# A two-layer decoder on one core: where probabilities, masks and three-part products are computed, and in what order

## The reference

```python
# layer 0: 16 heads of 64
normed = x * rsqrt(mean(x*x) + 1e-6) * norm_w
q, k, v = heads(normed @ wq), heads(ctx @ wk), heads(ctx @ wv)
x = x + (softmax(q @ k.T) @ v) @ wo              # 77 keys, 1024 columns into wo
# layer 1: 16 heads of 16
h = attention(ln1(x), ln1(x), causal=True);  x = x + h @ m_proj + b
h = attention(ln2(x), ctx,    causal=False); x = x + h @ c_proj + b
x = x + relu(ln3(x) @ f_w1 + f_b1) @ f_w2 + f_b2   # 1024 hidden
```

## Time and profile before

| | |
|---|---|
| median of three runs | 5340.66 us |
| profiled execution, its time | 5337.84 us |
| its span | 5336.1 us |
| PE busy | 5106.7 us, 96%, 48328 instructions |
| ACT busy | 4342.2 us, 81% |
| DVE busy | 2212.1 us, 41% |
| POOL busy | 536.4 us, 10% |
| granted TensorE clock, mean | 0.993 |

### The profile page before, as it was taken

The page is one execution under the profiler, slowest core; times in us unless marked ns, Lnnn a source line. Parts: engine busy times, 40 slices in busy tenths (PEclk is TensorE's granted clock), DMA queues, the critical chain, the costliest instruction groups (busy, mean ns, idle before and its releaser), DMA issues.

```text
span 5336.1 us, 138120 instructions
## 1 busy us (share of the span) xinstructions
PE 5106.7 (96%) x48328; PEld 4133.6 (77%) x48328; DVE 2212.1 (41%) x5823; ACT 4342.2 (81%) x17665; POOL 536.4 (10%) x845
## 2 busy tenths in 40 slices
PE   6999999999999999999999999999999999999996
PEld 5777777787787777777777777877777777777775
DVE  3444444443444444444444444434444444444442
ACT  3888888888888888888888888888888888888884
POOL 0001011111111011010110111110110100101100
PEclk9999999999999999999999999999999999999998
DMA  2000000000000000000000000000000000000000
GB/s 76 12 8 14 13 8 13 13 8 13 12 9 13 10 11 13 8 13 13 8 14 13 8 14 13 8 13 10 11 13 8 13 13 8 14 13 7 14 8 5
DMA packets 64257, 67.10 MB, mean 13 GB/s; under 512 B 4593, under 2 KB 62769, under 8 KB 63921
## 3 DMA queue, kind: packets, MB, share of 16 engines
q1 hardware_dynamic: 63920, 64.19, 3.9%
HBM read 47.40 MB, written 16.78 MB: 12 GB/s over the span
## 4 chain that ended last, share of the span: by engine, by line
PE 62%; ACT 24%; DVE 6%; issue 6%; DMA 0%; DVEq 0%; POOL 0%; ACTq 0%; SPq 0%; PEldq 0%; PEld 0%; POOLq 0%
PE ps L876 17%; ACT ps L480 15%; PE ps L841 6%; PE ps L843 5%; PE ps L842 5%; PE ps L1048 5%; PE ps L1031 4%; ACT coT L575 3%; PE ps L1020 3%; PE ps L929 3%; PE ps L1009 2%; PE ps L997 2%; PE ps L939 2%; PE ps L1015 2%; ACT v L460 2%
## 5 line engine op out<-in xcount | busy, mean ns | idle before, releaser
L480 ACT ACTIVATE ps<-ps,negmax 128x77 f32<-128x77 f32 (+2 forms) x6144 | 2076.8, 397 | 197.0 <-DVE negmax L701 195.4
L480 ACT ACTIVATION_READ_ACCUMULATOR ps<-ps,negmax 128x1 f32 x6144 | 1617.6, 275 | 0.8
L701 DVE TENSOR_REDUCE negmax<-ps 128x4 f32<-128x308 f32 (+2 forms) x1792 | 923.5, 563 | 765.8 <-PE ps L939 381.3
L433 POOL TENSOR_TENSOR small<-small 128x1 f32<-128x1 f32 (+1 forms) x448 | 260.9, 582 | 4608.3 <-DVE small L675 2305.7
L696 DVE TENSOR_TENSOR zTl<-ps,zTh 128x256 fp32r<-128x256 f32 x512 | 199.3, 420 | 898.0 <-ACT zTh L460 898.0
L876 PE MATMUL ps<-wf,coT 128*128 128x256 f32 x2048 | 475.8, 386 | 46.4 <-ACT coT L575 46.4
L876 PEld LDWEIGHTS ps<-wf,coT 128*128 128x128 f32 x2048 | 379.8, 190 | 127.0 <-issue 80.2
L876 PE MATMUL ps<-wo,coT 128*128 128x256 f32 x2048 | 475.9, 385 | 0.0
L557 ACT ACTIVATE probs<-ps 128x512 f32<-128x512 f32 x768 | 394.9, 601 | 70.1 <-PE ps L1020 70.1
L876 PEld LDWEIGHTS ps<-wo,coT 128*128 128x128 f32 x2048 | 378.6, 190 | 66.7 <-issue 10.3
L549 ACT ACTIVATE probs<-ps 77x512 f32<-77x512 f32 x512 | 275.5, 588 | 182.2 <-PE ps L981 179.1
(11 more groups left out here) (181 smaller groups left out, 10798.5 us busy)
## 6 DMA issues: line engine op xcount, KB each, us to landing
xin<-x_dram SPq DMA_DIRECT2D x64, 256.0 KB, 2.7
x<-x_dram SPq DMA_DIRECT2D x64, 256.0 KB, 2.7
out<-xr SPq DMA_DIRECT2D x64, 256.0 KB, 2.3
cin<-ctx_dram SPq DMA_DIRECT2D x64, 77.0 KB
wk<-wk_dram SPq DMA_DIRECT2D x1, 1024.0 KB, 5.1
wo<-wo_dram SPq DMA_DIRECT2D x1, 1024.0 KB, 7.9
wf<-f_dram SPq DMA_DIRECT2D x1, 1024.0 KB, 10.3
probs<-wq_dram SPq DMA_DIRECT2D x1, 1024.0 KB, 9.6
```

The costliest lines, as they stand in the source:

```text
L433: nc.gpsimd.tensor_tensor(rstd[:, stage, ts], veps[:, stage, ts], minus_half[:, ts], ALU.pow).then_inc(rstd_ready[stage], 1)
L480: ins = nc.scalar.activation(scores, scores, ACT.Exp, bias=negmax[w][:, t, h:h + 1], accum_out=sums[w][:, t, h:h + 1])
L701: nc.vector.tensor_reduce(dst, bank(s)[:, 0:heads * width].rearrange("p (h k) -> p h k", h=heads), AX_X, ALU.max, negate=True).then_inc(ma ...
```

## The change

Six things change together.

1. Layer 0. `qs0` keeps its exponentials: once ACT has them and their sums, DVE takes the reciprocals of the four sums (128x4) and multiplies the 4x77 probabilities by them, out of PSUM into SBUF. A new step `tr0.t.g` turns four heads over on PE (four transposes of 128x77) and ACT copies them. `ln.0`, `mt.0` and `sk0` are gone.
2. Causal masks. PE's mask matmuls are gone; DVE adds `causal` or `causalT` into the bank in place, and the maxima (by query) or ACT's exponentials (by key) wait for that.
3. `wo` and `f2` become three-part products (24 fp32r matmuls a tile instead of 8 fp32 ones). `pv0`'s result is split by ACT (high) and DVE (low). `h` moves from ACT to DVE: a maximum for the high part, a maximum and subtraction for the low part; `f_b1` is folded in by the bound `minus_bias` and a changed last row of biases.
4. The two weights, in two parts each, share one place in SBUF. Their parts are made at the start, stored to DRAM, and loaded from there in turn, by POOL: 2 MB after `f2` of a turn, 2 MB after `wo`.
5. Each step names its banks. ACT and DVE have orders of their own, in which single banks of a step can stand apart.
6. SP issues its transfers in the turn's order; the last full turn is written out behind the loop.

The diff, cut to its core:

```diff
+pv.1.1:3 rms+ qs0.0.3-:7 qs0.1.3-:6 proj.1.0:0 proj.1.1:4 tr0.1.1-:3 stat.2.0 tr0.1.0-:0 v0.1-:2 stat.2.1
+...
+        def load_parts(kind):
+            n = "wo0" if kind == "wo" else "f2"
+            nc.gpsimd.dma_start(tail_h[:], parted[n][0]).then_inc(tail_in[kind], 16)
+            nc.gpsimd.dma_start(tail_l[:], parted[n][1]).then_inc(tail_in[kind], 16)
+        pool.wait_ge(parts_out, 64)
+        load_parts("wo")
...
+                    if n in ("wo", "f2") and (n, 1 - step[1]) in c.seen:
+                        done = {s: v for st in order if st[0] == n for s, v, _ in c.of[st]["bank"]}
+                        for s, v in done.items():
+                            pool.wait_ge(full[s], v)
+                        ...
+                            load_parts(later[0])
...
+            def mask(u, r, heads, tile, at, added):
+                s, v, _ = u["bank"][r]
+                dve.wait_ge(full[s], v)
+                scores = bank(s).rearrange("p (h k) -> p h k", h=heads)[:, :, at:at + P]
+                nc.vector.tensor_tensor(scores, scores, tile[:].unsqueeze(1).to_broadcast([P, heads, P]),
+                                        ALU.add).then_inc(added, 1)
...
                     elif n == "qs0":
+                        if r == 0:
+                            maxima(u, 0, negmax[0][:, t, hs], 4, S)
+                            continue
+                        dve.wait_ge(summed_up, u["summed"][0][2])
+                        link(u, 0, nc.vector.reciprocal(over[:, t, hs], sums[0][:, t, hs]))
+                        nc.vector.tensor_tensor(rows_of_four(t, g)..., bank(s)..., over[...], ALU.mult).then_inc(free[s], 1)
...
-                        for s, _, _ in u["bank"]:
-                            diagonal = bank(s).rearrange("p (h k) -> p h k", h=heads)[:, :, 512 // heads - P:]
-                            pe.matmul(diagonal, identb[:], causal[:]..., start=False, stop=True, ...)
...
-                    elif n == "sk0":
-                        ...
+                    elif n == "tr0":
+                        for j in range(4):
+                            ins = pe.transpose(bank(s)[0:S, j * P:(j + 1) * P], rows_of_four(t, g)[:, j * S:(j + 1) * S],
+                                               ident[:])
...
+            def tail_product(u, th, tl, t):
+                for k in range(M0):
+                    ins = three(bank(s)[:, 0:C], th[:, k, ts], tl[:, k, ts], tail_h[:, k, :], tail_l[:, k, :],
+                                k == 0, k == M0 - 1)
+                    elif n == "h":
+                        ins = nc.vector.tensor_scalar(hTh[:, k, :], bank(s)..., minus_bias[:, k:k + 1], None, ALU.max)
+                        ins = nc.vector.scalar_tensor_tensor(out=hTl[:, k, :], in0=bank(s)..., scalar=minus_bias[:, k:k + 1],
+                                                             in1=hTh[:, k, :]..., op0=ALU.max, op1=ALU.subtract)
```

More of the change, by code:

```diff
@@ L44 @@
[L44 to L48, removed]
@@ new lines @@
+turn.1.0 turn.1.1 sk2.0/0 sk2.0/3 sk2.0/1 sk2.1/1 sk2.0/2 sk2.1/3 sk2.1/0 sk2.1/2 q1.1 pv.2.0 pv.2.1 k1 ck cv
+ctx qsA/2 turn.3.0 q0.2 qsA/0 k0.1 turn.3.1 qsA/3 qsA/1 qsB.1/3 qsB.1/1 k0.0 qsB.1/2 qsB.1/0 qs0.0.0 q0.1
+qsB.0/3 qsB.0/0 qsB.0/1 qsB.0/2 tr0.0.0 ln.1 qs0.0.1 v1 v0.0 mt.1 qs0.1.1 tr0.0.1 qs0.0.2 skB/3 skB/0 skB/2
+skA.0/3 skA.0/2 skA.0/0 skA.0/1 skB/1 qs0.1.0 qs0.1.2 pv.1.0 skA.1/0 skA.1/3 skA.1/2 skA.1/1
+"""
+DVE_ORDER_TEXT = """
+rms pv.1.1 qs0.0.3/0 qs0.1.3/0 proj.1.0 proj.1.1 stat.2.0 qs0.0.3/1 stat.2.1 norm.2.0 qs0.1.3/1 norm.2.1
@@ new lines @@
+norm.0 pv0.1 turn.2.0 turn.2.1 pv0.0 turn.0 qs2.1/3 pv0.2 qs2.1/0 qs2.1/2 qs2.1/1 pv0.3 qs2.0/3 qs2.0/2
+qs2.0/1 qs2.0/0 wo.0 stat.1.0 norm.1.0 wo.1 stat.1.1 ln.2 norm.1.1 turn.1.0 turn.1.1 pv.2.0 pv.2.1 proj.2.0
+stat.3.0 proj.2.1 stat.3.1 norm.3.0 qsA/m2 qsA/2 qsA/m0 ctx qsA/0 norm.3.1 qsA/m3 turn.3.0 qsA/m1 qsA/3 qsA/1
+turn.3.1 qsB.1/m3 qsB.1/m1 qsB.1/3 qsB.1/1 qsB.1/m2 h.3/0 h.3/1 qsB.1/2 qsB.1/m0 qsB.1/0 qsB.0/m3 qsB.0/m0
+qs0.0.0/0 qsB.0/m1 qsB.0/m2 qsB.0/3 qsB.0/0 qs0.0.0/1 qsB.0/1 qsB.0/2 h.2/0 h.0/0 qs0.0.1/0 h.0/1 h.2/1 ln.1
@@ L135, in next @@
-    def next(self, step):
[L136 to L154, removed]
+        self.after = after
+        self.of = {step: {"place": k, **{r: [None] * n for r, n in USES[step[0]].items()}} for k, step in enumerate(order)}
+        self.seen = set()
+        for ring, given in signals(order).items():
+            at = [0] * RINGS[ring]
+            for step, j, s in given:
+                at[s] += 1
+                value, total = before[ring][s] + at[s], sum(before[ring]) + sum(at)
+                if per_turn is not None:
+                    value = turn * per_turn[ring][s] + value
+                    total = turn * sum(per_turn[ring]) + total
+                self.of[step][ring][j] = (s, value, total)
@@ L156, in source @@
+    def next(self, step):
+        self.seen.add(step)
+        return self.of[step]
     def source(self, step, reader):
@@ L381, in _ @@
             sp.dma_start(cin[0:S, :], ctx[0]).then_inc(c_in, 16)
[L382 to L400, removed]
```

406 lines of the change are left out of this document (250 added, 156 removed).

## The result

| | before | after |
|---|---|---|
| median | 5340.28 us (4 runs, 5338.04 to 5346.11) | 5738.24 us (4 runs, 5733.14 to 5740.97) |
| span of the profiled execution | 5336.1 us | 5731.0 us |
| mean granted clock | 0.993 | 0.944 |
| a turn (mean of 55, start of `xin`'s transposes to the next) | 81.10 us | 87.39 us |
| first such start | 56.7 us | 77.1 us |

The kernel after takes 1.074 times as long, 95% interval 1.0724 to 1.0761. Forecast were 5190 us in a range of 5020 to 5390: wrong in sign and outside the range. By the table, 62 turns that are 6.3 us longer are 390 us, and the start is 20 us more.

A forecast was written before the change was run, and what follows sets the result against it. PE alone set the old period; after the change, chains across three engines loaded to three quarters or more would decide. 5337.8 - 180 (turns) + 32 (start) = 5189.8, with 2.8 for the median 5193, said as 5190 us; range 5020 to 5390.

The forecast's parts named there:

- five stretches of the prediction: One turn cut at four places, waits between engines followed in each: 13.4 + 1.2 + 33.3 + 15.0 + 15.3 = 78.2 us.
- The loads in the loop cost nothing while they land in time: 2 MB has 19 us from `f2.1` to `wo.0`, some 45 from `wo.1` to `f2.0`, so no cost.
- The sum of PE's work: PE's busy time per turn: 79.1 - 4.4 - 3.6 - 3.4 - 0.3 + 3.9 = 71.5 us.
- The tails: Four `wo` and `f2` tiles on PE: 24 three-part matmuls take 2.8 us against 3.65 a tile, saving 3.4 a turn.
- `mt.2`'s 2.6 us: Ahead of `mt.2`, ACT's chain takes 13.4 us against 10.8 of PE work, so PE stands 2.6 us.
- that DVE paces it: Between `sk2` and `mt.1`, 20.1 us of unbroken DVE work sets 33.3 us; PE waits at four places, under 1 us each.
- 0.61 and 0.37: Time in us of one DVE mask over 512 and 256 columns; a turn's masks add 10.8 us.
- VectorE as the bound: Rival: masks cost 0.35 us more each, 4.2 in the long stretch; turn 82.6, total 5466 us; chance 0.17.
- the late weights: Rival: two loads take 22.8 against 19 us, PE stands 3.8 at `wo.0`; turn about 82, total 5429; chance 0.05.
- The start: Set-up before the loop: parting and storing two weights in turn, 36.8 us less some 5, adds 32 (20 to 45).
- the prediction's figure of 6.8: In the start, the Trainium skill's time in us for 2 MB, by which the start would cost 26.
- The clock rival: 24 transposes in a row lower PE's clock each turn, losing 1.7 us; 5190 + 105 = 5295 us; chance 0.12.

The follow-up runs named there:

- repaired: Kernel after plus 64 semaphore instructions ahead of PE's loop, where PE waits for constants, and `wo`'s load issued at `stat.2.1`: 5229.5 us, 0.978 of the kernel before.
- plain kernel: Repaired kernel with `wo` and `f2` as plain fp32 products kept in SBUF, no loop loads or low parts: 5265.5 us; with no extra instructions 5249.6, with 34 5372.1.
- the four kernels that are fetched anew: Kernel after, 5738.24 us; after with 192 extra PE instructions, 5643.0; plain kernel with 34, 5372.1; kernel before with 192, 5444.2.

## Why the prediction was wrong, step by step

PE's turn in the five stretches of the prediction, mean of 55 turns in us, with the time that PE stands in them:

| stretch | forecast | after | repaired | stands, after / repaired |
|---|---|---|---|---|
| `qs2.1` to `mt.2` | 13.4 | 13.6 | 13.7 | 1.4 / 1.3 |
| `mt.2` to `sk2` | 1.2 | 1.0 | 1.0 | 0.1 / 0.2 |
| `sk2` to `mt.1` | 33.3 | 33.6 | 33.7 | 1.9 / 1.9 |
| `mt.1` to `pv.1.1` | 15.0 | 18.3 | 16.3 | 2.5 / 0.6 |
| `pv.1.1` to `qs2.1` | 15.3 | 20.9 | 14.4 | 5.0 / 0.5 |
| turn | 78.2 | 87.4 | 79.1 | 10.9 / 4.5 |

- **The step that failed** is a tacit one: that instructions are at hand. The prediction counted the work of each engine and the waits on semaphores, and nothing for the way of PE's 1641 records to PE. In its last two stretches, 2.0 and 5.0 us of the jump's stall appear. With the fetches gone the turn is 81.1: they cost 6.3 us a turn, 5.0 in standing and the rest in slower work behind it at the lower clock (62 x 6.3 = 390 us). No row of before showed it; its 19 packets of q8 only told that there the loop was not fetched.
- **"The loads in the loop cost nothing while they land in time"** failed as well. They land in time, but the store behind them does not, and through POOL's list it delays `norm.2.1`. With the load moved the turn falls from 81.1 to 79.0: 2.1 us, 130 us in all, a part of it clock. The prediction asked whether the loads are late themselves, and not what small transfer stands behind them.
- The sum of PE's work was low: without its waits PE takes 74.5 in the repaired kernel. (The terms of the prediction's line add up to 71.3; its 71.5 is the sum of the work in its five stretches.) `sk0` gave 4.8 (said 4.4), masks 3.5 (3.6), transposes cost 3.6 (3.9). The tails gave 2.2 and not 3.4: `wo`'s 3.65 was the longest of the four tiles (3.37 to 3.65), and a three-part tile takes 2.9 to 3.0. The remaining 2.4 us are hand-overs inside matmul groups that waits stretch, such as `qs2`'s 32 matmuls (+1.0).
- The waits came to 4.5 and not 6.7, so the sum, 79.1, is 0.9 over the forecast's 78.2. `mt.2`'s 2.6 us are 0.8, since more work lies in front of it; the stretch's 13.4 stands at 13.6. The 33.6 for the stretch's forecast of 33.3 is in part luck. PE's work in it is 31.8 and not 30.3, its waits 1.9 and not 3.0, and that DVE paces it is not borne out: in the plain kernel, which has no low parts of `h`, DVE is busy for 90% of the piece behind `qsA`, in the repaired one for 98%, and the stretch takes 33.7 in both.
- VectorE: a mask has a mean of 0.692 us for 512 and 0.423 for 256 columns, tails of 0.05 to 0.08 included, so 0.61 and 0.37 hold as distances. 56.5 us against 57.4. Two rivals had the right sign, VectorE as the bound (5466) and the late weights (5429), and both named the wrong mechanism: the masks cost what was said, and the weights of the kernel after lie ready at least 15.8 us ahead of `wo.0`.

Masks in the kernel after, by shape:

```profile
L810 DVE TENSOR_TENSOR ps<-ps,causal 128x256 f32<-128x256 f32 x512 | 198.6, 422 | 3.8 <-PE ps L1106 3.8
...
L810 DVE TENSOR_TENSOR ps<-ps,causal 128x512 f32<-128x512 f32 x256 | 177.1, 692 | 7.7 <-PE ps L1103 6.4
```

- The start: +20.3 us against +32. Parting takes 4.5 us and not 5.9. The pairs of stores, which SP issues (the prediction's figure of 6.8 is for a transfer of POOL's), take 6.4 and 7.3 and not 10. ACT's first instruction comes at 69.5 and not near 80. The end of the chain (DVE's first and second parting, ACT's first instruction, POOL's first load):

```profile
53.17 2.77 DVE L728 SCALAR_TENSOR_TENSOR tail_l<-probs,tail_h 128x256 fp32r<-128x256 f32 x8
62.38 1.71 DVE L720 CAST tail_h<-probs 128x256 fp32r<-128x256 f32 x8 [6.43 <-DMA parted_wo<-tail_l]
```

```profile
69.54 1.28 ACT L690 ACT_TABLE_LOAD   x1 [69.54 <-DVEq L761]
```

```profile
74.24 0.73 POOL L535 DMA_DIRECT2D tail_h<-parted_wo  x1 [69.85 <-DMA parted_f<-tail_l]
```

- The clock rival: the clock did fall in each turn, but behind the stall at the jump, not behind 24 transposes.

Put together, with 12 us less for the start than forecast: 5193 + 62 x (87.4 - 78.2) - 12 = 5751, against 5738 measured. Of the 9.2 us a turn, 6.3 are the fetches, 2.1 the store behind the load and 0.9 the rest.

The Trainium skill, Runtime: NRT & Kernel Launch, section "Instruction fetch mechanics", says that PE's instruction memory takes 2048 instructions in blocks of 256, and that a taken branch to a target outside the window costs a fetch. The 16 KB packets and a border every 256 records agree with it. But 2048 instructions are 8 blocks, and here a loop that touches 8 was fetched again, so the limit lies one block lower than that number suggests. It also says that prefetch is purely sequential; read alone, that would have loops of 1600 instructions fetched always, and here they ran without a single fetch wherever they touched 7 blocks.

## What to carry to other kernels

Before an edit changes the length or the beginning of a long loop, look at the instruction queues' packets in the page: if there are none inside the loop, ask how near the loop is to being fetched anew, and test it with idle instructions ahead of it, at several shifts: in the kernel before, 64 and 128 showed nothing and 192 did. When a loop grows new transfers, list every small transfer that can be queued behind them and who waits for it. A count that gives the busy time of ACT and DVE to a microsecond, as here, still says nothing of a wait that no semaphore shows.

## What the runs showed of the hardware that was not expected

- A PE loop of 1576 to 1689 records runs with no fetch at all, with nine fetches of 16 KB a turn, or with nine in every second turn, by the place at which it begins: 79.5 us a turn without and 83.8 with fetches in the plain kernel, 81.1 against 87.4 in the kernel after.
- Without loads the fetches come in every second turn (281 and 286 packets in 62 turns), with loads in every turn (565).
- PE stands at the first border of a block behind the jump, wherever it lies: after 23, 86, 21 and 63 records of the loop in the four kernels that are fetched anew.
- A fetch that meets a 2 MB load takes longer: a gap of 5.15 us with the load issued at the jump, 2.23 with it issued later. With 192 extra instructions, where the border comes 86 records behind the jump, the mean gap is 2.7 us with the load at its old place.
- 256 KB issued right behind a 2 MB load land 8.6 to 9.6 us after their issue; ahead of it, or without it, 2.3 to 2.8.
